# A selective-scan block with a gated feed-forward on one core: the first half's z block 0 computed beside x_proj, its down steps ended before the switch, its last state multiplied by C in channel layout

## The reference

```
xn = layernorm(x)
xi, z = split(xn @ in_proj_w)                 # 1024 channels each
xc = silu(causal_conv4(xi) + conv_b)
dt_r, B, C = split(xc @ x_proj_w.T)           # 32 + 16 + 16 columns, each rmsnormed
dt = softplus(dt_r @ dt_proj_w.T + dt_bias)
for each token t, channel d, state n (16 of them):
    h[d,n] = exp(dt[t,d] * A[d,n]) * h[d,n] + dt[t,d] * B[t,n] * xc[t,d]
    y[t,d] += C[t,n] * h[d,n]
s = ((y + D_param * xc) * silu(z)) @ out_proj_w.T
g = silu(ffn(xn))                             # gate, up (1376 wide), down: 4-bit codes
                                              # times a scale, plus a rank-32 term each
out = x + s * g
```

## Time and profile before

| what | us |
|---|---|
| median of 3 runs (lowest, highest) | 1154.04 (1153.87, 1154.09) |
| the profiled execution | 1153.82 |
| its span in the trace | 1151.7 |
| PE busy (share of the span) | 1103.5 (96%) |
| DVE busy | 926.9 (80%) |
| POOL busy | 734.7 (64%) |
| ACT busy | 674.3 (59%) |

### The profile page before, as it was taken

One profiled execution on the slowest core, in us unless ns is written; L12 is line 12 of the kernel. 1 busy time (PEld: TensorE's weight loads), 2 busy tenths in 40 slices (PEclk: granted clock), 3 DMA queues, 4 the chain that ended last, 5 costly groups with the idle time before them and its releaser, 6 DMA issues.

```text
span 1151.7 us, 12396 instructions
## 1 busy us (share of the span) xinstructions
PE 1103.5 (96%) x4366; PEld 589.5 (51%) x4366; DVE 926.9 (80%) x741; ACT 674.3 (59%) x850; POOL 734.7 (64%) x406
## 2 busy tenths in 40 slices
PE   5998999999999999999999899999999999999998
PEld 3443455555545555554443335555555455555543
DVE  4897999999789999996315469999987899999820
ACT  3224577877647777764022357777775477777410
POOL 2000799999537999980410048999983599999311
PEclk9998999999999999999999899999999999999999
DMA  7663289999914999999411124999984289998941
GB/s 248 218 205 128 100 206 235 249 243 225 247 54 118 241 238 261 209 201 315 174 37 36 46 82 130 239 238 250 240 205 149 84 207 247 242 238 193 280 181 43
DMA packets 62162, 215.44 MB, mean 187 GB/s; under 512 B 6762, under 2 KB 6890, under 8 KB 61588
## 3 DMA queue, kind: packets, MB, share of 16 engines
q0 software_dynamic: 16128, 88.09, 38.8%
q1 hardware_dynamic: 44388, 120.88, 30.9%
q10 hardware_dynamic: 1584, 5.68, 1.2%
HBM read 103.56 MB, written 22.98 MB: 110 GB/s over the span
## 4 chain that ended last, share of the span: by engine, by line
POOL 39%; PE 28%; issue 19%; DVE 11%; ACT 2%; DMA 1%; POOLq 0%; DVEq 0%; SPq 0%
POOL ub L627 34%; PE psM L1076 8%; PE psM L1015 6%; DVE hb L1253 5%; POOL yT L637 5%; PE psA L845 4%; PE psM L876 3%; PE psT L991 2%; DVE xc L1244 1%; DVE th L1103 1%; PE psA L961 1%; DMA yT<-yc 1%; DVE xc L1103 1%; DVE hid L1103 1%; PE psT L840 1%
## 5 line engine op out<-in xcount | busy, mean ns | idle before, releaser
L627 POOL TENSOR_TENSOR ub<-dtx,bn 128x1024 f32<-128x1024 f32 x256 | 647.0, 2590 | 275.0 <-DMA bn<-ss_rows_scratch 187.3
L1253 DVE TENSOR_TENSOR_SCAN hb<-psA,ub 128x1024 f32<-128x1024 f32 x256 | 581.7, 2280 | 26.4 <-POOL ub L627 23.2
L732 ACT ACTIVATE psA<-dt,cc 128x1024 f32<-128x1024 f32 x256 | 285.9, 1119 | 139.9 <-DVE hb L1253 138.0
L876 PE MATMUL psM<-xnT,w_ts 128*126 128x512 f32 x704 | 328.8, 598 | 3.5 <-DVE th L1103 3.5
L991 PEld LDWEIGHTS psT<-ident,hb 128*128 128x128 f32 x1984 | 226.9, 141 | 166.0 <-issue 82.5
L991 PE MATMUL psT<-ident,hb 128*128 128x128 f32 x1984 | 270.9, 275 | 13.1 <-DVE yT L1103 7.3
L753 ACT ACTIVATE yc<-psT,ssm 128x512 f32<-128x512 f32 x336 | 216.9, 679 | 20.9 <-PE psT L991 13.2
L876 PEld LDWEIGHTS psM<-xnT,w_ts 128*126 128x126 f32 x704 | 122.8, 190 | 114.8 <-issue 114.8
L1015 PE MATMUL psM<-w_dn,hid 126*128 126x512 f32 x352 | 163.3, 594 | 0.0
L1004 PE MATMUL psM<-xnT,w_ts 128*128 128x512 f32 x256 | 121.4, 593 | 0.0
L637 POOL DMA_DIRECT2D yT<-yc x112 | 111.2, 993 | 8.6 <-ACT yc L753 5.2
(11 more groups left out here) (85 smaller groups left out, 576.6 us busy)
## 6 DMA issues: line engine op xcount, KB each, us to landing
yT<-yc POOLq DMA_DIRECT2D x112, 768.0 KB, 8.4
bn<-ss_rows_scratch SPq DMA_DIRECT2D x66, 512.0 KB, 7.1
w_ts<-w_gu_scratch SPq DMA_DIRECT2D x44, 504.0 KB, 5.3
w_ts<-w_in_dram SPq DMA_DIRECT2D x32, 256.0 KB, 5.1
hb<-z_scratch SPq DMA_DIRECT2D x16, 512.0 KB, 7.3
z_scratch<-hid SPq DMA_DIRECT2D x28, 256.0 KB, 6.7
w_gu_scratch<-hid ACTq DMA_DIRECT2D x11, 504.0 KB, 5.1
yT<-x_dram SPq DMA_DIRECT2D x8, 512.0 KB, 8.9
```

The costliest lines, as they stand in the source:

```text
L627: pool.tensor_tensor(ub[:, i % 2, :], dtx[:, i, :], bn[:, t, :], ALU.mult).then_inc(s_u, 1)
L732: act.activation(psA[:, i % 2, :], dt[:, i, :], ACT.Exp, scale=negA[:, h * DH + i, bass.ds(n, 1)]).then_inc(s_a, 1)
L876: mm = pe.matmul(psM[0:IM, gu, :], w_ts[:, off % 2, at:at + IM], xnT[:, k, h * CH:(h + 1) * CH], start=(k == 0), stop=(k == HK - 1))
L1253: dve.tensor_tensor_scan(hb[:, t * DH + i, :], psA[:, i % 2, :], ub[:, i % 2, :], 0.0, ALU.mult, ALU.add).then_inc(s_scan, 1)
```

## The change

The diff below is cut: renamed or re-indexed lines, semaphores, and the second table of SP are left out.

1. z block 0 of each first half leaves the list of steps (`TILES[0]` has no `("z", 0)`). Its matmuls are `z0_step`: four steps ahead of `x_proj(7)`, one behind it, three behind the transposes of its result. Its weights are loaded during the conv stage into the free upper part of a slot, ACT makes the two copies (`copy_z0`) that the stores need, and the first halves have their own list of steps and their own order on SP. Only one step of gate tile 0 instead of two runs inside the x_proj chain; the other seven run before row 0.
2. All down steps of the first half are in its loop: 123 steps in the first 60 quarters, 9 in the last 4. ACT's copy of the fourth down block stays behind the switch's silu.
3. Row 15 of the first half is no longer transposed or added to `yT`. DVE multiplies the four states by the C row (`times_c`) and adds them to xc*D (`last_state`), as in the second half; there the four `times_c` now also stand ahead of the four `last_state`. SP loads the C row in both halves, and the load of the next half's B row 0, which takes the same buffer, waits for the fourth `times_c`.
4. In the switch the order is new on PE (gate tiles 0 and 1 between the `turn_back`), on DVE (`drive(1, 3)` first, silu_gate and hidden earlier) and on ACT (tanh of tile 0 before the third decay).

```
-REST = 6
-ROWS = [NS, NS - 1]
-TURNED = 127
+ROWS = NS - 1
+TURNED = [123, 127]
 def steps_of(p, h):
-    if h == 0:
-        steps, at, n = STEPS[:-REST], p, QUARTERS
-    elif p < QUARTERS - 4:
-        steps, at, n = STEPS[:TURNED], p, QUARTERS - 4
+    steps = STEPS[h]
+    if p < QUARTERS - 4:
+        steps, at, n = steps[:TURNED[h]], p, QUARTERS - 4
     else:
-        steps, at, n = STEPS[TURNED:], p - (QUARTERS - 4), 4
+        steps, at, n = steps[TURNED[h]:], p - (QUARTERS - 4), 4
...
+SP_END = [("z", 3, 0), ("F", 0), ("B", 13), ("z", 3, 1), ("w",), ("B", 14), ("B", 15), ("d", 0, 0), ("C",),
+          ("d", 1, 0), ("N", 0), ("W",), ("back",), ("F", 1), ("g", 0), ("d", 2, 0), ("N", 1), ("d", 3, 0), ("g", 1), ("g", 2)]
...
                     def load_b(n, t, h=h):
                         sp.wait_ge(s_u, unit(b, h, n, 0) + 4)
-                        if n == 0 and h == 0 and b > 0:
-                            sp.wait_ge(s_hc, b * DH)
+                        if n == 0 and b + h > 0:
+                            sp.wait_ge(s_hc, blk(b, h, 0))
...
+                def copy_z0(c):
+
+                    t = TH_SLOTS["z", 0, c]
+                    act.wait_ge(s_z0, 2 * b + c + 1)
+                    act.wait_ge(s_ths[t], th_stored(b, 0, t, -1))
+                    act.activation(th_tiles[t], psA[:, 0, c * CH:(c + 1) * CH], ACT.Copy).then_inc(s_late, 1)
+
+                copy_z0(0)
                 act.wait_ge(s_xp, b + 1)
                 act.activation(xr, psM[:, 0, :], ACT.Copy).then_inc(s_xr, 1)
...
                 act.activation(rs[:, 0:1], mv[:, 0:1, 1], ACT.Softplus).then_inc(s_past, 1)
+                copy_z0(1)
...
+                for k in range(HK):
+                    z0_step(0, k)
                 x_proj(DB - 1).then_inc(s_xp, 1)
+                z0_step(1, 0)
...
-                gate_up(b, 0, 0, 0)
+                for k in range(1, HK):
+                    z0_step(1, k)
...
-                        for i in range(2):
+                        for i in range(DH):
                             turn_back(i)
-                            for kind, j, k in STEPS[len(STEPS) - REST + i * REST // 2:len(STEPS) - (1 - i) * REST // 2]:
-                                down(h - 1, j, k)
-                        for i in range(2, DH):
-                            turn_back(i)
-                            gate_up(b, h, 0, i - 2)
-                        for q in range(2, 4):
-                            gate_up(b, h, 0, q)
-                    for n in range(1, FILL):
+                            if i < 2:
+                                gate_up(b, h, 0, 2 * i)
+                                gate_up(b, h, 0, 2 * i + 1)
+                            else:
+                                gate_up(b, h, 1, 2 * i - 4)
+                                gate_up(b, h, 1, 2 * i - 3)
+                    for n in range(1 + h, FILL):
                         ahead(n)
...
-                        if h < HALVES:
-                            stt(xc[:, m, :], xc[:, m, :], cc[:, m, DP:DP + 1], psT_row, ALU.mult, ALU.add).then_inc(s_ybr, 1)
-                        else:
-                            dve.wait_ge(s_ym, b * DH + i + 1)
-                            dve.tensor_tensor(xc[:, m, :], xc[:, m, :], psT_row, ALU.add).then_inc(s_ybr, 1)
+                        dve.wait_ge(s_ym, k + 1)
+                        dve.tensor_tensor(xc[:, m, :], xc[:, m, :], psT_row, ALU.add).then_inc(s_ybr, 1)
...
+                    def times_c(i):
+
+                        dve.wait_ge(s_crow, 16 * (b * HALVES + h) + 16)
                         dve.wait_ge(s_scan, unit(b, h, NS - 1, i) + 3)
                         dve.tensor_tensor(hb[:, DH + i, :], hb[:, DH + i, :], bn[:, 0, :], ALU.mult).then_inc(s_hc, 1)
...
+                        if p == QUARTERS - 4:
+                            for i in range(DH):
+                                times_c(i)
+                        if n == ROWS:
                             last_state(q)
```

More of the change, by code:

```diff
@@ L116 @@
 Y_ORDER = [2, 0, 3, 4, 5, 1, 6, 7]
-def y_order(n):
-    return list(range(TB)) if n == NS - 1 else Y_ORDER
-def y_pos(n, tb):
-    return y_order(n).index(tb)
-TD_HALF = [(NS - 1) * YD + TB, (NS - 1) * YD]
+TD_HALF = ROWS * YD
 TC_HALF = (NS - 1) * YA
@@ L356, in landed, with use @@
         def landed(b, off):
-            return b * (8 * W_USES) + 16 * (off // 2 + 1)
+            return 16 * (w_use(b, off) // 2 + 1)
         def w_half(h, n):
-            return DB + h * W_HALF + n
-        def use(kind, i):
-            return TILES.index((kind, i))
+            return DB + h * len(TILES[0]) + n
+        def use(h, kind, i):
+            return TILES[h].index((kind, i))
         def gated(b, h, n, gu):
@@ L538, in _ @@
                         load_b(1, 1)
-                    for what in SP_ORDER:
+                    for what in SP_ORDER[h]:
                         if what[0] == "B":
@@ L542, in _ @@
                         elif what[0] == "G":
-                            off = w_half(h, use("g", what[1]))
-                            load_g(what[1], off, off % 2)
+                            off = w_half(h, use(h, "g", what[1]))
+                            load_g(what[1], off, w_slot(b, off))
                         elif what[0] == "N":
@@ L818, in _ @@
                         for tb in Y_ORDER[2 * q:2 * q + 2]:
-                            if n < ROWS[h] and not by_dve(n, tb):
+                            if n < ROWS and not by_dve(tb):
                                 scale_y(n, tb)
-                    for what in ends(QUARTERS - 1, h):
-                        copy_late(h, *what)
+                    if h + 1 == HALVES:
+                        for what in ends(QUARTERS - 1, h):
+                            copy_late(h, *what)
                 for i in range(DH):
@@ L868, in gate_step @@
                 gu, k = divmod(step, HK)
-                off = w_half(h, use("g", n))
+                off = w_half(h, use(h, "g", n))
+                t = w_slot(b, off)
                 if step == 0:
-                    pe.wait_ge(s_w[off % 2], landed(b, off))
+                    pe.wait_ge(s_w[t], landed(b, off))
                 if k == 0 and (h or n):
@@ L1307, in _ @@
                     else:
+                        drive(1, 3)
                         add_skip(0)
                         times_z(0)
-                        drive(1, 3)
                         add_skip(1)
                         scan(0, 0, 0)
+                        silu_gate(0, 0)
                         times_z(1)
                         add_skip(2)
+                        hidden(0, 0)
                         scan(0, 0, 1)
```

171 lines of the change are left out of this document (95 added, 76 removed), and 7 rows, old and new, of the table SP_ORDER.

## The result

The changed kernel took 1144.42 us (median of 4 runs, 1143.22 to 1145.42) against 1153.99 (1153.87 to 1154.09): a ratio of 0.9919, 95% interval 0.9907 to 0.9931. Its profiled execution took 1143.22 us with a span of 1141.4; the span before was 1151.7. Measured a second time, the same kernel gave 1142.13 (1140.38 to 1143.19), ratio 0.9902 (0.9890 to 0.9915). The forecast was 1142.6.

What follows compares the result with a forecast made beforehand. PE's queue was taken to bound the switch, with PE, DVE and POOL nearly full in the first half's rows. 1153.8 - 10.8 (two switches) - 0.6 (x_proj) = 1142.4, forecast 1142.6 us as median; range 1136.5 to 1149.

Steps and rivals of the forecast that it cites:

- What bounds the switch: Switch between halves: PE's queue sets it; last scan to row 1's first scan falls from 47.9 to about 42.5 us.
- Its sign of being wrong: Switch: the forecast is wrong if DVE waits there for a B row or a z block; no size given.
- The ends: Switch, second half's first scan: 320.6 if DVE keeps the port, 323.3 if DVE and POOL alternate.
- The middle, 322.0: Switch: start taken for the second half's first scan, because no row decided who gets the port.
- Rival (a): Switch: DVE keeps the port and POOL steps aside until add_skip; about 7.4 us per switch, 1138.4 us; chance 0.20.
- Row 0 and row 1: Second half, first scan to row 1's first scan: 17.6 us plus one port meeting of 1.9, 19.5; was 23.45.
- cost at nothing: First half's rows: fewer PE steps, DVE and POOL work the same, so still about 179.7 us.
- rival (c): Switch: SP's list becomes the wait, the second half's B row comes late; 1153.2 us, no change; chance 0.05.
- Rival (d): First half's rows: closer gate tiles no longer fit, each half loses up to 9.6 us; 1161.8 us; chance 0.05.
- (b): Around x_proj: the low clock stays and the chain is 1.7 us later per batch; 1146.4 us; chance 0.15.
- the gain of the chain: x_proj: z steps fill PE's wait and keep the clock up; 0.3 us gained per batch, 0.6 in all.
- the late end of the range: Whole kernel: both switches at their late end, 8.2 us gained, with the low clock's 3.4 lost: 1149.2 us.

Runs made afterwards that it cites:

- the added product: Changed kernel with one more POOL product per switch, released while DVE runs times_c, last_state and drive without a gap: 1148.56 us, ratio 0.9964.
- POOL waiting: Changed kernel with POOL's first product of the second half waiting for DVE's last drive instead of its first: 1139.18 us; further kernels on that chip keep this wait.
- the kernel with the down steps behind: Changed kernel with the first half's last six down steps behind the first two turns back, three each: 1143.08 us, ratio 0.9904.

## Why the prediction was right, and where it was off

**What bounds the switch: right.** PE's queue set it, DVE had the time, and the work taken off PE came out of the stretch: 6.6 us per switch in one profile and 4.8 in the other, where 5.4 were forecast, with the gate steps 16.4 us behind the last scan (forecast 315.0, or 16.0). The forecast gave the parts of the change no prices of their own; the down steps, ended ahead, did not help but cost 1.4 us per switch. Its sign of being wrong that DVE waits for a z block came by the letter, with the 0.41 us of times_z(0), at no cost.

**The port: the term was mis-sized by taking the middle.** The ends were the right ones: counted from the last scan as in the earlier trace rows, the first scan was forecast at 320.6 if DVE keeps the port and at 323.3 if the two alternate, and the profiles have 321.1 and 322.9. The middle, 322.0, occurred in neither. The B row was taken to land 4.7 us behind its issue, or 11.4 behind the last scan, which by the table is the early case; it took 5.9 and 5.6 us in the first profile, 5.4 and 4.8 in the second. Rival (a) is the first profile; the second shows the alternation. Its argument, that DVE's instructions follow without a gap, is refuted by the added product.

**Row 0 and row 1.** 19.5 us were forecast for row 0, one meeting of 1.9 included; 19.25 came, with the meeting at the place named. Row 1, 0.9 us shorter in both batches, was not in the sum.

**The first half's rows: "cost at nothing" failed in one profile.** It argued with the steps on PE and the work of DVE and POOL, and these did not change: with B rows in time the half takes 179.9 to 180.6 us, in the two kernels with the z block undone 179.7 to 180.3. The new SP list was weighed only at the switch, as rival (c). Of the 3.7 us of the first profile 2.8 are the wait for a B row. It was asked for 4.5 to 4.9 us after its buffer was free in all fourteen batches with this list, and in thirteen it was in time. So the list took the slack, and one landing of 9.9 us, which is not explained, did the rest. Rival (d) is refuted: the closer gate tiles cost 0.9 us at most.

**x_proj.** The clock stayed up, as forecast, so (b) is refuted; x_proj(7) took 1.08 us where the earlier trace rows has 1.97. What failed is the path behind it: the forecast took the gain of the chain for a gain of the rows. Counted from the silu of block 7, the first drive comes 0.6 us earlier with the z block than without it (13.49 against 14.09 us in the first batch). But POOL's first product, and with it the first scan, waits for the first B row. The changed kernel, then the one with the z block undone:

```profile
120.01 4.66 POOL L636 TENSOR_TENSOR ub<-dtx,bn 128x1024 f32<-128x1024 f32 x2 [102.86 <-DMA bn<-ss_rows_scratch]
```
```profile
118.11 4.66 POOL L625 TENSOR_TENSOR ub<-dtx,bn 128x1024 f32<-128x1024 f32 x2 [101.73 <-DMA bn<-ss_rows_scratch]
```

And the issues of that row, in the same order:

```profile
bn<-ss_rows_scratch SPq DMA_DIRECT2D x1, 512.0 KB, 4.8
```
```profile
bn<-ss_rows_scratch SPq DMA_DIRECT2D x1, 512.0 KB, 3.8
```

The row is asked for 0.6 us earlier and takes 0.9 longer to land; why was not found. From that silu to the first scan are 22.8 to 23.0 us in the eleven profiles with the z block and 22.55 in the three without it, so the block costs 0.25 to 0.45 us in the first batch. In the second batch it is 22.8 to 23.0 against 23.07 and 22.93. The 0.6 us gained in all did not come.

**Sums.** Rival (b)'s loss per batch, 5.1 less 3.13, is 2.0 us and not 1.7, so (b) and the late end of the range belong some 0.5 us later. POOL's busy time in the two switches before differs by 0.13 us, not 0.02. Neither changes the forecast.

The forecast missed the first measurement by 1.8 us and the second by 0.5. That it came so close is in part luck: in the first profile a larger saving than forecast and the late row nearly cancelled, and in the second the switches saved less than forecast while row 1, which was not in the sum, gave 0.9 us in each batch.

## What to carry to other kernels

When an engine's wait is taken away, look at what ran in that wait unhindered: here POOL's products did, and they now fight for DVE's port, so that a landing 0.2 us earlier makes the switch 1.8 us longer. Where two engines share a port, start the one with time to spare in the other's next pause. And when loads are put in another order, compare for each one the moment its buffer is free with the moment it is asked for, in the whole list, not only at the place that the change is about.

## What the runs showed of the hardware

An earlier operand can cost time: a B row that lets POOL start 12.4 us or less behind the last scan costs 1.8 us more than one that comes after 12.6. Four kernels on one chip had it land 5.7 to 5.9 us behind its issue, always late enough; three on another 4.8 to 5.4, always too early; on a third, with POOL waiting, it was 5.0 to 5.7. Whether chip or execution decides stays open.

Why a drive went ahead of a POOL product that had come during an undelayed last_state (twelve times of twelve), while a last_state let a product in that had come during a drive (six of six), was not found. The slower single times of the kernel with the down steps behind, 6 us above its profiled one, were not profiled either; two of them have a mean granted clock of 0.996 where the profiled one has 0.999.
